# Softmax attention: scores in two pairs of PSUM banks, maxima in three single banks, sums inverted and maxima turned on VectorE

## What is computed

```
q, k, v = split_heads(binlinear(xn, Wq, bq)), ..k.., ..v..      # 8 x 16 x 512 x 8
att = softmax(einsum('bhtd,bhsd->bhts', q, k) * 8 ** -0.5)
y = einsum('bhts,bhsd->bhtd', att, v) -> 8 x 512 x 128
s = binlinear(y, Wp, bp)
```

## Time and profile before

| | us |
|---|---|
| runs | 982.49, 989.87, 992.93 (median 989.87) |
| the profiled execution | 992.35 |
| its span | 990.5 |
| granted clock of TensorE, mean share of full | 0.957 |
| attention's first reduction of maxima starts | 32.1 |
| its last reduction ends | 411.3 |
| its last exponential ends | 430.7 |

### The profile page before, as it was taken

How to read it: one execution, slowest core, us unless ns; L and a number is a source line. 1 busy time by engine, 2 the same in 40 slices (tenths; PEclk the granted TensorE clock), 3 DMA queues, 4 the chain that set the end, 5 groups by cost and what they waited for, 6 DMA issues and landing times. The chain is left out here.

```text
span 990.5 us, 18391 instructions
## 1 busy us (share of the span) xinstructions
PE 897.2 (91%) x6674; PEld 461.9 (47%) x6674; DVE 695.5 (70%) x1054; ACT 634.7 (64%) x1383; POOL 366.1 (37%) x355
## 2 busy tenths in 40 slices
PE   4699999999999999979998989899769999999997
PEld 2333444344434344448888878332223444444443
DVE  7879888898989999613333338878867767766654
ACT  4468677778777878852322222476557778777875
POOL 4013030214343333005556542255645547554300
PEclk9579899999999999989999989999789999999999
DMA  7615525140414000036766553259977999999800
GB/s 226 250 39 207 230 71 211 40 162 27 176 45 151 28 26 25 8 98 181 209 198 199 164 176 96 54 111 136 144 88 75 108 110 101 103 104 112 92 12 22
DMA packets 80973, 114.30 MB, mean 115 GB/s; under 512 B 12946, under 2 KB 58004, under 8 KB 78452
## 3 DMA queue, kind: packets, MB, share of 16 engines
q1 hardware_dynamic: 73684, 94.87, 48.2%
q0 software_dynamic: 6352, 17.86, 5.3%
q10 hardware_dynamic: 848, 0.40, 0.1%
HBM read 56.00 MB, written 33.57 MB: 90 GB/s over the span
## 5 line engine op out<-in xcount | busy, mean ns | idle before, releaser
L989 DVE TENSOR_REDUCE a_nmax<-quad 128x2 f32<-128x1024 f32 x256 | 302.1, 1220 | 32.4 <-PE quad L603 29.9
L798 ACT ACTIVATE a_probs<-bank 128x512 f32<-128x512 f32 x339 | 190.8, 598 | 53.0 <-PE bank L620 36.9
L1873 ACT ACTIVATE a_late<-quad 128x256 f32<-128x256 f32 (+3 forms) x512 | 180.4, 461 | 37.3 <-PE quad L1642 36.6
L2028 DVE SCALAR_TENSOR_TENSOR a_late<-a_late,const 128x512 f32<-128x512 f32 x128 | 117.8, 928 | 73.8 <-ACT a_late L1873 73.5
L632 PE MATMUL av<-a_probs,a_va 128*32 128x256 f32 x2048 | 166.1, 397 | 0.9 <-ACT a_probs L798 0.6
L603 PE MATMUL quad<-k_stack,q_stack 24*128 24x512 f32 x512 | 133.6, 523 | 9.9 <-DVE a_nmax L989 5.8
L620 PE MATMUL bank<-q_stack,k_stack 26*128 26x512 f32 x339 | 136.8, 504 | 2.8 <-DMA q_stack<-a_nparts 2.0
L798 ACT ACTIVATE a_probs<-misc 128x512 f32<-128x512 f32 x173 | 103.4, 598 | 28.9 <-PE bank L620 16.2
L1642 PE MATMUL quad<-q_stack,k_stack 96*128 96x256 bf16 (+3 forms) x512 | 104.1, 305 | 7.4 <-ACT a_late L1873 3.7
L1653 PE MATMUL av<-a_late,a_va 128*32 128x512 f32 (+3 forms) x1024 | 96.1, 448 | 8.1 <-DVE a_late L2039 7.1
L508 POOL DMA_INDIRECT sorted_rows<-x_rows,a_slot x64 | 62.4, 974 | 107.5 <-PE av L632 105.0
(11 more groups left out here) (304 smaller groups left out, 1406.1 us busy)
## 6 DMA issues: line engine op xcount, KB each, us to landing
spread<-a_parts SPq DMA_DIRECT2D x48, 256.0 KB
q_stack<-a_parts SPq DMA_DIRECT2D x96, 128.0 KB, 7.4
k_stack<-a_parts SPq DMA_DIRECT2D x96, 128.0 KB, 7.8
wu<-packed_weights SPq DMA_DIRECT2D x20, 384.0 KB
m_wu<-packed_weights SPq DMA_DIRECT2D x19, 384.0 KB
q_stack<-spread SPq DMA_DIRECT2D x7, 1024.0 KB
k_stack<-spread SPq DMA_DIRECT2D x7, 1024.0 KB
sorted_rows<-in_shape_constants POOLq DMA_DIRECT2D x5, 1040.0 KB, 5.4
```

The costliest lines, as they stand in the source:

```text
L798: act.activation(probs[:, (GH * s + j) % 8, :], col_bank(n)[:, :], ACT.Exp, scale=scale).then_inc(col_free, 1)
L989: dve.tensor_reduce(nmax[quad % 2][:, at:at + 2 * TT:TT], row_slot(n)[:, :, :], AX_X, ALU.max, negate=True)\
L1873: act.activation(probs[:, (64 * b + n) % 12, kt * P:T], quad[:, n % 4, kt * P:T], ACT.Square, bias=1.0, scale=0.25)\
L2028: dve.scalar_tensor_tensor(out=blocks, in0=blocks, scalar=1.0, in1=S["tri"][:, None, :].broadcast_to([P, GH, P]), op0=ALU.add, op1=ALU.mul ...
```

## The change

- The four banks of `quad` become two pairs for "units": scores (two heads a unit) and all side jobs, in the order of PE's work. ScalarE reads all of them but the last batch's gathers and projection: the exponentials as two instructions of 2 x 512 columns a step, and now also gathers, projections, logits and counts by copies. A unit waits until the unit two before it has been read.
- The three single banks hold maxima only. Each bank is filled by one matmul and read by one reduction of 512 columns (512 instead of 256 reductions). AHEAD is 6 instead of 8.
- Every fourth step VectorE transposes `nmax` (now 128 x 32) in blocks of 32 x 32 into `ntop`, right behind the first reduction of the next four steps' group (behind all of them for the last quad). PE's turn and the split into two parts go; the maximum is one row of the stack, and scores have 25 contraction rows. `max_rows` issues four DMAs of 16 x 128 bytes instead of eight. ScalarE's four DMAs for the first quad go.
- `weigh` is one group of four matmuls of 512 columns and stands between the first maxima and the second scores; side jobs stand last in the step.
- VectorE inverts the gathered sums from SBUF (`invert_sums`, one step after the gather); POOL multiplies (`scale_rows`, t = 2 and 4, semaphore `yn_done`, for which PE's transposes of y wait at t = 5) and adds the bias (`add_bias`, t = 8). The last batch is divided and read by VectorE as before.

The diff, cut to its core (what is left out renames semaphores and banks):

```diff
-        nmax = [sb(f"nmax{i}", [P, P]) for i in range(2)]
-        nparts = sb("nparts", [DQ1, 2, P], F32R)
+        nmax = [sb(f"nmax{i}", [P, STRIP]) for i in range(2)]
+        ntop = [sb(f"ntop{i}", [P, STRIP]) for i in range(2)]
+        gathered = sb("gathered", [P, 2, NCOMP])
...
-        score_banks = (S["bank"][0], S["bank"][1], S["misc"])
+        max_banks = (S["bank"][0], S["bank"][1], S["misc"])
...
-        AHEAD = 8
+        AHEAD = 6
         STACK = 16 * 2
         WRITES = 16 * 2 * len(HALVES)
-        ROWS = 16 * 2 * GH
+        ROWS = 16 * GH
...
+        def pair_of(n):
+
+            return S["quad"][:, 2 * ((n - SINGLES) % 2):2 * ((n - SINGLES) % 2) + 2, :]
+
+        def bank_of(n):
+
+            return S["quad"][:, n % 4, :] if n < SINGLES else pair_of(n)[:, 0, :]
+
+        def wait_bank(engine, n):
+
+            if n < SINGLES:
+                wait(engine, unit_read, n - 3)
+            elif n < SINGLES + 2:
+                wait(engine, unit_read, SINGLES)
+            elif units[n - 2][0:2] == ("gather", B - 1):
+                wait(engine, last_read, units[n - 2][2] + 1)
+            else:
+                wait(engine, unit_read, n - 1)
...
-                wait(sp, row_free, row_no["turn", quad, 0] + 1)
-                for i in range(2 if quad else 1):
-                    for j in range(GH):
-                        row = STRIP * j + HROWS + i
-                        sp.dma_start(qs[b % 4][row:row + 1, c, :], nparts[TT * j:TT * (j + 1), i, :].bitcast(F32))\
-                          .then_inc(rows_in[quad % 2], 16)
+                wait(sp, turned, quad + 1)
+                rows = qs[b % 4][HROWS:HROWS + STRIP * (GH - 1) + 1:STRIP, c, :].rearrange("r (t q f) -> r t q f", t=TT, q=P // STRIP)
+                for q in range(P // STRIP):
+                    sp.dma_start(rows[:, :, q, :], ntop[quad % 2][STRIP * q:STRIP * q + TT * GH, :]).then_inc(rows_in[quad % 2], 16)
...
+            def scale_rows(b, u):
+                wait(pool, rec, 2 * b + u + 1)
+                if u == 0 and b >= 1:
+                    wait(pool, unit_mm, unit_no["y", b - 1, 0] + 1)
+                pool.tensor_tensor(yn[:, 2 * u:2 * u + 2, :].rearrange("p k (h d) -> p k h d", d=DH),
+                                   gathered[:, :, 0:C].rearrange("p k (h d) -> p k h d", d=DH),
+                                   rden[:, u, :, :, None].broadcast_to([P, 2, H, DH]), ALU.mult).then_inc(yn_done, 1)
+
+            def add_bias(b):
+                wait(pool, unit_read, unit_no["proj", b, 0] + 1)
+                rows = S["s"][:, TT * b:TT * (b + 1), :]
+                pool.tensor_tensor(rows, rows, S["bp"][:, None, :].broadcast_to([P, TT, C]), ALU.add)
...
             def maxima(m, i):
-                n = row_no["max", m, i]
                 quad, qt = m // TT, m % TT
                 b, c = quad // NG, quad % NG
                 if m == 0 and i == 0:
                     wait(pe, first_quad, STACK)
                 if (m == TT or (m % 16 == 0 and m > 0)) and i == 0:
                     wait(pe, stacked[b % 2], STACK * (b // 2 + 1))
-                wait(pe, row_free, n - 1)
                 for k in range(2):
+                    n = GH * m + 2 * i + k
                     r = 2 * (1 - i) + k
                     at = slice(STRIP * r, STRIP * r + HROWS)
-                    last = pe.matmul(row_slot(n)[:, k, :], qs[b % 4][at, c, qt * P:(qt + 1) * P].bitcast(F32R),
-                                     ks[b % 4][at, c, :].bitcast(F32R), start=True, stop=True)
-                last.then_inc(row_mm, 1)
-
-            def turn(quad):
-                n = row_no["turn", quad, 0]
-                wait(pe, row_free, max(n - 1, row_no["max", TT * quad + TT - 1, 1] + 1))
-                pe.transpose(row_slot(n)[:, 0, 0:P], nmax[quad % 2][:, :], S["ident"]).then_inc(row_mm, 1)
-
-            def score(s, j):
-                n = col_no["s", s, j]
+                    wait(pe, max_free, n - 2)
+                    pe.matmul(max_banks[n % 3][:, :], qs[b % 4][at, c, qt * P:(qt + 1) * P].bitcast(F32R),
+                              ks[b % 4][at, c, :].bitcast(F32R), start=True, stop=True).then_inc(max_mm, 1)
+
+            def scores(s, i):
+                n = unit_no["s", s, i]
                 quad, kt = s // TT, s % TT
                 b, c = quad // NG, quad % NG
-                if kt == 0 and j == 0:
+                if kt == 0 and i == 0:
                     wait(pe, rows_in[quad % 2], ROWS * (quad // 2 + 1))
-                wait(pe, col_free, n - 2)
-                at = slice(STRIP * j, STRIP * j + HROWS + 2)
-                pe.matmul(col_bank(n)[:, :], ks[b % 4][at, c, kt * P:(kt + 1) * P].bitcast(F32R),
-                          qs[b % 4][at, c, :].bitcast(F32R), start=True, stop=True).then_inc(col_mm, 1)
-
-            def weigh(s, part):
+                wait_bank(pe, n)
+                for k in range(2):
+                    j = 2 * i + k
+                    at = slice(STRIP * j, STRIP * j + HROWS + 1)
+                    last = pe.matmul(pair_of(n)[:, k, :], ks[b % 4][at, c, kt * P:(kt + 1) * P].bitcast(F32R),
+                                     qs[b % 4][at, c, :].bitcast(F32R), start=True, stop=True)
+                last.then_inc(unit_mm, 1)
+
+            def weigh(s):
 
                 b, c, kt = s // 16, s % 16 // TT, s % TT
-                if part == 0:
-                    wait(pe, col_free, col_no["s", s, GH - 1] + 1)
-                    if kt == 0 and c % 2 == 0:
-                        wait(pe, o_read, 2 * b + c // 2)
-                at = slice(T // 2 * part, T // 2 * (part + 1))
+                wait(pe, unit_read, unit_no["s", s, 1] + 1)
+                if kt == 0 and c % 2 == 0:
+                    wait(pe, o_read, 2 * b + c // 2)
                 for j in range(GH):
-                    last = pe.matmul(av[STRIP * j:STRIP * (j + 1), at], va[b % 2][:, kt, GH * j + c, :],
-                                     probs[:, (GH * s + j) % 8, at], start=(kt == 0 and c % 2 == 0 and part == 0),
+                    last = pe.matmul(av[STRIP * j:STRIP * (j + 1), :], va[b % 2][:, kt, GH * j + c, :],
+                                     probs[:, (GH * s + j) % 8, :], start=(kt == 0 and c % 2 == 0),
                                      stop=(kt == TT - 1 and c % 2 == 1), skip_group_check=True)
-                if part == 1:
-                    last.then_inc(av_mm, 1)
+                last.then_inc(av_mm, 1)
...
                 b, t = s // 16, s % 16
-                score(s, 0)
-                score(s, 1)
+                scores(s, 0)
                 if s + AHEAD < LAST:
                     maxima(s + AHEAD, 0)
                 if s >= 1:
-                    weigh(s - 1, 0)
-                score(s, 2)
-                score(s, 3)
+                    weigh(s - 1)
+                scores(s, 1)
                 if s + AHEAD < LAST:
                     maxima(s + AHEAD, 1)
...
-            def exps(s):
-                for j in range(GH):
-                    n = col_no["s", s, j]
-                    if j == 0:
-
-                        wait(act, av_mm, s - 1)
-                    wait(act, col_mm, n + 1)
-                    act.activation(probs[:, (GH * s + j) % 8, :], col_bank(n)[:, :], ACT.Exp, scale=scale).then_inc(col_free, 1)
...
+            def exps(s, i):
+                n = unit_no["s", s, i]
+                if i == 0:
+
+                    wait(act, av_mm, s - 1)
+                wait(act, unit_mm, n + 1)
+                at = (GH * s + 2 * i) % 8
+                act.activation(probs[:, at:at + 2, :], pair_of(n), ACT.Exp, scale=scale).then_inc(unit_read, 1)
...
+            def read_gathered(b, u):
+                n = unit_no["gather", b, u]
+                wait(act, unit_mm, n + 1)
+                wait(act, yn_done, 2 * b + u)
+                act.activation(gathered[:, :, :], bank_of(n)[:, 0:2 * NCOMP].rearrange("p (k n) -> p k n", k=2), ACT.Copy).then_inc(unit_read, 1)
+
+            def read_projected(b):
+                n = unit_no["proj", b, 0]
+                wait(act, unit_mm, n + 1)
+                act.activation(S["s"][:, TT * b:TT * (b + 1), :], bank_of(n).rearrange("p (t c) -> p t c", t=TT), ACT.Copy).then_inc(unit_read, 1)
...
+            def maximum(m, k):
+                n, quad, qt = GH * m + k, m // TT, m % TT
+                at = TT * ((k + 2) % GH) + qt
+                wait(dve, max_mm, n + 1)
+                dve.tensor_reduce(nmax[quad % 2][:, at:at + 1], max_banks[n % 3][:, :], AX_X, ALU.max, negate=True).then_inc(max_free, 1)
+
+            def turn(quad):
+                wait(dve, max_free, GH * TT * (quad + 1))
+                wait(dve, rows_in[quad % 2], ROWS * (quad // 2))
+                dve.transpose(ntop[quad % 2][:, :], nmax[quad % 2][:, :]).then_inc(turned, 1)
+
+            def maxima(m):
+                maximum(m, 0)
+                if m % TT == 0 and m > 0:
+                    turn(m // TT - 1)
```

(7 more changed lines are left out.)

395 lines of the change are left out of this document (183 added, 212 removed).

## The result

The changed kernel takes **1032.88 us** (median of 4 runs, 1027.27 to 1035.98) against 989.68 us of the kernel before (4 runs, 982.49 to 992.93). The ratio is 1.044 (95% interval 1.036 to 1.052): 43 us slower, where 970 us, 20 less, was forecast, and outside the range of 948 to 1003.

What follows compares the result with a forecast made beforehand. VectorE was taken to bound the attention stage, less moments when TensorE hands it nothing. Savings of 9.7 (VectorE's work), 5 (idle) and 6 (tail) made 21 us off 992.35, so 971.5; 970 us was predicted, range 948 to 1003.

Steps and rivals of the forecast that it cites:

- Reductions of 512 columns: VectorE's maxima: 512 short reductions 0.60 us apart replace 256 long ones at 1.135, +16.6 us (bounds +11.5 and +57.6).
- Rival E, the fixed cost: Short reductions on PSUM hardly overlap and start every 0.66 us: 31 us more, about 1001 us; chance 0.08.
- Block transposes: On VectorE, 31 splits of the maxima (21.4 us) go; transposes at 0.20 us each add 6.2.
- ScalarE, GpSimd, reciprocals: 1024-column exponentials take 1.03 us and ScalarE fits; GpSimd's products and bias sums stay hidden; divisions becoming reciprocals give -6.3 us.
- Values in one group: 0.47 us.: TensorE's value matmuls as one group of four with 512 columns would take 0.47 us a step and fit.
- Rival D: Lockstep: TensorE, serving reductions and exponentials in one order, costs 0.2 us a step, 24 in all: about 995 us; chance 0.18.
- The clock: Half clock in the attention stage: 10 us of VectorE idle time, for the opening and two short later stretches.
- Rows: Row transfers with AHEAD 6: late by 1.4 us a block, plus 4 us for quads sharing the queue with bulk transfers.
- rival C: Rows come late, each quad pays in full, 32 x the lateness: 1002 us at 1 us beyond 3.7; chance 0.15.
- Idle of VectorE: VectorE's idle time between first and last reduction: 35 us against 40.2 before, a term of -5 us.
- Tail: From last reduction to last exponential: 6 steps of 2.14 us plus 0.6, 13.4 instead of 19.4 us, -6 us.
- B, the ring runs free: Maxima banks no longer shared with side jobs: VectorE idle 14 to 18 us instead of 35, about 952 us; chance 0.17.

Runs made afterwards that it cites:

- two parts and AHEAD 8: Changed kernel with the values split again into two parts of 256 columns and AHEAD 8 instead of 6: 995.2 us against 993.9 before.
- the two pairs of runs with AHEAD 6 and 8: AHEAD 6 against 8: changed kernel with values in two parts, 1009.6 and 995.2 us; kernel before with block transposes, 995.3 and 982.4 us.
- the kernel with two parts: Changed kernel with the values again in two parts of 256 columns, the second at the step's end, AHEAD 6: 1009.6 us; with extra matmuls 1029.8 us.

## Why the prediction was wrong, point by point

The forecast took 21 us off a span of 990.5; the measured span is 1025.5, 56 us more than that. By place: VectorE's idle time between first and last reduction is 70 us instead of 35 (35 us), its work fell by 4.3 instead of 9.7 (5), the tail took 21.2 instead of 13.4 (8), and behind the last exponential, where nothing was forecast, the program takes 566.8 instead of 559.8 us (7), with 51 us of half clock there instead of 37.

- *Reductions of 512 columns*: +16.6 forecast, 0.60 us apart; measured 0.60 and +12 to +15. Right. Rival E, the fixed cost (0.66), is refuted. By the Trainium skill's 125 ns of access overhead on PSUM (Perfetto Trace Analysis, Optimizing Scalar/DVE Operations) they would stand, by the prediction's estimate, 0.665 us apart. The traces do not agree.
- *Block transposes*: 0.20 us forecast and measured; alone they shorten the stage by 15 us and the time by 11.
- *ScalarE, GpSimd, reciprocals*: exponential 1.03 forecast, 1.02 measured; products 0.64 and bias sums 1.29 us, hidden. Right. VectorE's busy time fell by 4.3 us instead of 9.7: a reduction that had to wait does not overlap the one ahead (0.68 instead of 0.60 us), and there are 110 such waits (72 and 38) against 55 in the earlier trace rows. With two parts and AHEAD 8 it fell by 12.7.
- *Values in one group: 0.47 us.* **This is the step that failed.** It measured 1.00. From it came "value matmuls fit", the tail's step of 2.14, and the small chance of lockstep. Split again, the group gives back 23 us with AHEAD 6 and 33 with AHEAD 8; merged in the kernel before, it costs 47. Rival D had the mechanism, exponentials and reductions served in one order, but priced it at 0.2 us a step, without the clock.
- *The clock*: 10 us of idle time were allowed, for the opening and two short stretches as before. **No term and no rival let the change lower the clock itself.** At full clock the steady blocks are no longer than before (46.4 to 47.0 against 47.4); the 2.74 us steps leave TensorE gaps, and what follows runs at 0.50. By the scale above the clock is some 30 of the 35 us between the spans, and also all that the split gives back with AHEAD 8.
- *Rows*: the sum held 15 us for them (1.4 a block and 4 for the bulk transfers); the two pairs of runs with AHEAD 6 and 8 give 14 and 13 to 16. The size was right, but it lay hidden behind the lump, where the waits for the rows sum to 8.1 us (10 to 20 forecast, over 40 for rival C, which is refuted as the main cause). With AHEAD 8 the same pieces of 128 bytes were never waited for. The Trainium skill (DMA: Bandwidth & Descriptors, Specifications) has transfers below 512 bytes done as read-modify-write; what that costs no run here tells apart from the shorter lead.
- *Idle of VectorE, and the premise under it*: 35 forecast, 70 measured; 52 with two parts and AHEAD 8. The sum counted each us of work taken from VectorE as one us of time. With the block transposes alone that held: 13.9 us less work, the stage 14.7 shorter. With two parts and AHEAD 8 it did not:
```profile
32.30:410.70 378.40, 368.43 (x3211) 162.85 (x3215) 326.30 (x589) 281.82 (x326) 116.86 (x131) 0.95 0.29 104
```
VectorE is busy for 12.7 us less than in the earlier trace rows and idle for 11.9 us more, and the stage is only 0.8 us shorter; TensorE is busy for 368.43 us of it, 6.9 more than before.
- *Tail*: 13.4 forecast, 21.2 measured, at a clock of 0.55 and 3.78 us a step at the end.
- *Start*: step 0's exponentials at 51.26 instead of near 49, 0.2 us earlier than before: nothing gained.
- *B, the ring runs free*: refuted; its waits are longer than before (64.1 us against 29.9).

What stays open: with both causes gone the change is even (995.2 to 993.9), and not the 21 us faster that was forecast. Transposes (-11) and short reductions (+12 to +15) leave 1 to 4 us, so the divisions and readings taken from VectorE, 11 us in the forecast, brought 3 at most in time. They did leave VectorE: its work is 339.0 before, +13.8 with short reductions, -13.9 with block transposes, and 326.3 with two parts and AHEAD 8, which leaves 12.6 for them. It came back as idle time behind TensorE. Whether the single banks, the pairs shared with the side jobs or the order of the step cause it, no run isolates. And the runs show that gaps on TensorE go before the clock's fall and filling them prevents it, not what exactly the throttle weighs.

## What to carry to other kernels

Find out what one record of a group row stands for before using its count: here a matmul left two, and a term was 0.5 us too small for it. Where one in-order engine feeds two others, write both loops down and keep the blocks that stand in them short; here, splitting one of 1.00 us in two was worth 23 to 33 us, and merging had saved 0.14 us of TensorE's time a step. When a change leaves TensorE more gaps, price the clock: at full clock the blocks were no longer than before, and some 30 us went with the clock. And check a repair by the mechanism, not only by the time: the split gave time back, but not in the steps where the loop said it would.

## What was not expected of the hardware

- Work added to TensorE made a kernel faster: 24 full-array matmuls of 512 columns that nobody reads, -15 us, with the granted clock kept up (half-clock time 170 to 116 us). In the kernel with two parts the same matmuls cost 20 us.
- One microsecond at half clock cost about 0.37 us here (0.30 to 0.45 by the runs of other kernels), the same kernel's spans going from 1080.7 to 1144.3 us.
- A change of order that takes no more of TensorE's time can move the granted clock from 0.959 to 0.882 (the kernel before with block transposes, values in two parts or as one group last). Of the 105 us between the two spans, the 176 us more of half clock are 65 by the scale; the rest goes with steps of 2.67 instead of 2.25 us.
